# A grouped convolution block on one core: the written orders of every engine and of the DMA queue merged anew

## The chip, the cores and the metric

The kernel runs on one core of a Trainium2 chip. The metric is the device time of one execution in microseconds, lower is better. The engines are TensorE (PE in the profile, its weight loads PEld), VectorE (DVE), ScalarE (ACT), GpSimd (POOL) and SyncE (SP), which here only issues DMAs.

## The reference

The input x is 16 samples of 64 x 64 pixels with 768 channels, f32 (201 MB). Each sample is normalised by groups of channels, projected to 16 channels, convolved by a mixture of four experts whose gates come from the pooled projection, expanded to 768 channels and added to x.

```python
xc = conv1x1(groupnorm(x, 32 groups), conv1_w, conv1_b)        # 768 -> 16 channels
h = mean(xc over pixels) @ H_w.T + H_b                         # 4 gates, the best 2 kept
g = softmax(where(top2, h, -inf))
for i in range(4):                                             # expert i: resize by 2**i, 3x3 conv, resize back
    experts.append(resize(conv3x3(resize(xc, 2**i), convl_w, convl_b), 1))
out = x + conv1x1(sum_i g_i * experts[i], conv2_w, conv2_b)    # 16 -> 768 channels
```

The resizes and the 3x3 convolution fold into one 3x3 convolution with its own taps at the edges. The gates of four samples come together (round r needs samples r, r+4, r+8, r+12 and gives the gates of samples 4r to 4r+3).

## The kernel before

A sample is 8 loads of 1536 KB (`L sample.i:slot`), each into one of 13 slots of `x_sb`; a slot has two halves of 768 KB. x is needed twice: for the statistics and the projection, and again when the result is added. A few loads of eight samples are kept (`KEPT`); the other halves are read a second time (`R sample.i.half:slot.half`). A half is stored by `S sample.i.half`. The queue SP issues the words of `TRANSFERS` one by one and in this order: 128 L, 172 R and 256 S, and waits before each for what it needs. An L or R into a slot whose last tenant was only read waits for PE's transposes of it (`transposed`), into a slot whose tenant was added to it waits until that store has landed (`stored`). An S waits for DVE's adds (`added`).

The work comes in two halves with an order of samples each, `A_ORDER` and `B_ORDER`, which the change leaves alone. A sample enters (A) by these works:

- B on DVE (line 881): statistics of 28 of the 32 groups, in four parts of two loads. S on ACT (lines 786 and 788): the other four groups of each part.
- Z on PE (line 676): four matmuls sum the statistics over the partitions, each once its part is there.
- F on DVE (lines 891 to 911), D on ACT (773): the fold, from the sums to the scaled weights `w1`.
- T on PE (line 651): 24 works of 8 transposes of 128 x 128, from the slots into PSUM; T.5, T.11, T.17 and T.23 free two slots each. T on ACT (line 769): the copy of such a work to SBUF.
- M on PE (line 664): 24 works of 4 matmuls, the projection of one copied work; M.0 waits for `w1`. I on ACT: the image to SBUF.

It leaves (B) by these:

- C on PE (line 716): seven parts of the convolution, with bands of taps that POOL writes. H on ACT and L on DVE: the result in two parts. X on PE and ACT: spread to the partitions.
- E on PE (line 747): 32 tiles of 128 pixels with 768 channels. A on DVE (line 960): the add of such a tile to x.
- G, H, P: the four rounds of gates.

T, E, X, Z and W share a ring of three PSUM buffers, and the copies of T go to three SBUF buffers; so T may run up to six works ahead of M. Every engine runs its works in a written order: `PE_ORDER`, `ACT_ORDER`, `DVE_ORDER`. In a word, `T8.2-5` stands for works 2 to 5 of sample 8. In a bracketed row of the trace a work T is 8 records, a work M is 8 as well, and Z is 8.

```python
            for work in parse_order(PE_ORDER):
                program_of[work[0]](*work[1:])
```

Of the kernel before, what the change touches and what calls it, by code (L numbers as in the profile page):

```python
# [8 lines left out]
ALU = mybir.AluOpType  # L9
# [25 lines left out]


# [23 lines left out]
R0.4.1:11.0 R0.5.0:11.1 R0.5.1:3.0 S0.3.0 S0.3.1 S0.4.0 R0.6.0:3.1 R0.6.1:4.0 R0.7.0:4.1 S0.4.1 S0.5.0 R0.7.1:11.0  # L60
S0.5.1 R4.0.0:11.1 S0.6.0 S0.6.1 R4.0.1:3.0 S0.7.0 R4.1.0:3.1 S0.7.1 R4.1.1:4.0 S4.0.0 R4.2.0:4.1 S4.0.1 R4.2.1:11.0
S4.1.0 R4.3.0:11.1 S4.1.1 R4.3.1:3.0 S4.2.0 R4.4.0:3.1 S4.2.1 R4.4.1:4.0 S4.3.0 R4.5.0:4.1 S4.3.1 R4.5.1:11.0 S4.4.0
R4.6.0:11.1 S4.4.1 R4.6.1:3.0 S4.5.0 R4.7.0:3.1 S4.5.1 R4.7.1:4.0 S4.6.0 S4.6.1 S4.7.0 L14.2:11 S4.7.1 L14.3:3 L14.4:4
S7.0.0 S7.0.1 S7.1.0 S7.1.1 S7.2.0 L14.5:2 S7.2.1 S7.3.0 L14.6:10 S7.3.1 L14.7:12 S7.4.0 S7.4.1 R5.0.0:6.0 S7.5.0
S7.5.1 S7.6.0 S7.6.1 S7.7.0 S7.7.1 L6.0:7 R5.0.1:6.1 S5.0.0 L6.1:1 L6.2:5 L6.3:0 R5.1.0:6.0 S5.0.1 L6.4:10 L6.5:12
R5.1.1:6.1 L6.6:2 L6.7:4 S5.1.0 L10.0:3 L10.1:11 S5.1.1 R5.2.0:6.0 L10.2:8 L10.3:9 R5.2.1:6.1 S5.2.0 L10.4:2 L10.5:4
R5.3.0:6.0 S5.2.1 L10.6:10 L10.7:12 R5.3.1:6.1 S5.3.0 L11.0:0 L11.1:5 R5.4.0:6.0 S5.3.1 L11.2:1 R5.4.1:6.1 S5.4.0
R5.5.0:6.0 S5.4.1 R5.5.1:6.1 S5.5.0 R5.6.0:12.0 R5.6.1:12.1 R5.7.0:6.0 S5.5.1 S5.6.0 S5.6.1 R5.7.1:6.1 S5.7.0
R6.1.0:12.0 R6.1.1:12.1 R6.2.0:6.0 S5.7.1 S6.0.0 S6.0.1 R6.2.1:6.1 S6.1.0 R6.3.0:7.0 S6.1.1 R6.3.1:7.1 S6.2.0
R6.4.0:12.0 S6.2.1 R6.4.1:12.1 S6.3.0 R6.5.0:6.0 S6.3.1 R6.5.1:6.1 R6.6.0:7.0 S6.4.0 R6.6.1:7.1 S6.4.1 S6.5.0 S6.5.1  # L70
R6.7.0:12.0 S6.6.0 R6.7.1:12.1 S6.6.1 L11.3:6 S6.7.0 L11.4:7 S6.7.1 S10.0.0 L11.5:12 S10.0.1 S10.1.0 S10.1.1 L11.6:3
# [917 lines left out]
```

## Time and profile before

| | us |
|---|---|
| median of 3 runs | 1488.0 (1486.47 to 1491.37) |
| the profiled execution | 1492.88 |
| its span, first to last instruction | 1491.2 |
| mean granted TensorE clock | 0.858 |
| moved by DMA | 540.01 MB, mean 362 GB/s |

The profile is of one execution. A row of the windows view gives for a stretch the busy time of PE, PEld, DVE, ACT and POOL, the granted clock of TensorE and the busy share of the DMA engines; a full DMA shows as 1.03, as from 1160 us on. A row of a timeline gives start, length, engine, line, operation and how many; the brackets behind it tell how long the engine sat idle before, and for whom.

### The profile page before, as it was taken

What the parts mean: (1) busy time and instruction counts of PE and PEld (TensorE: products, weight loads), DVE (VectorE), ACT (ScalarE), POOL (GpSimd) and SP (SyncE); (2) the same over time, 40 slices, a digit from 0 to 9 for tenths busy, and PEclk for the clock granted to TensorE, in tenths of its full rate; (3) what the DMA queues carried; (4) which work ended last, traced back from release to release, by engine and by line L of the source; (5) the groups of instructions that cost most, each with busy time, mean ns of one, the idle gap of its engine ahead of it and who ended that gap; (6) DMA issues with size and microseconds to landing.
All of it is one profiled execution on the core that took longest, in us unless ns stands there. A gap on an engine that the chain in (4) does not pass through costs nothing.

```text
span 1491.2 us, 24053 instructions
## 1 busy us (share of the span) xinstructions
PE 1191.8 (80%) x8700; PEld 833.8 (56%) x8700; DVE 1034.0 (69%) x2747; ACT 665.3 (45%) x1549; POOL 313.8 (21%) x381
## 2 busy tenths in 40 slices
PE   0688998998988689889986799879597898876853
PEld 0556776665655466656654577556465565644421
DVE  6778788678559877685496886449685855454843
ACT  2688887672433488625224784403270243100100
POOL 1082003403050000061440001065005003651000
PEclk9899999999997799979977899967798789976855
DMA  9788886499999978999999998999999999999999
GB/s 341 251 336 314 299 304 253 160 409 339 401 384 387 401 288 301 387 368 414 400 393 403 408 389 296 375 411 353 406 382 317 361 413 415 413 415 416 411 406 365
DMA packets 188162, 540.01 MB, mean 362 GB/s; under 512 B 12810, under 2 KB 12810, under 8 KB 188044
## 3 DMA queue, kind: packets, MB, share of 16 engines
q1 hardware_dynamic: 187772, 538.09, 93.7%
q8 instruction: 69, 1.13, 0.3%
q10 hardware_dynamic: 272, 0.39, 0.1%
q14 instruction: 49, 0.40, 0.1%
HBM read 337.12 MB, written 201.33 MB: 361 GB/s over the span
## 4 chain that ended last, share of the span: by engine, by line
PE 40%; DMA 31%; DVE 15%; SPq 5%; ACT 4%; issue 4%; DVEq 0%; ACTq 0%
DMA x_sb<-in_x 22%; PE ring_ps L651 17%; DMA out<-x_sb 9%; DVE x_sb L960 9%; PE img_ps L664 9%; PE conv_ps L716 7%; PE ring_ps L747 5%; DVE stats L881 3%; SPq L483 2%; SPq L493 2%; ACT xT L769 2%; SPq L486 1%; ACT unread_squares L786 1%; ACT unread_copy L788 1%; PE ring_ps L735 1%
## 5 line engine op out<-in xcount | busy, mean ns | idle before, releaser
L960 DVE TENSOR_TENSOR x_sb<-x_sb,ring_ps 128x768 f32<-128x768 f32 x512 | 460.0, 949 | 290.1 <-DMA x_sb<-in_x 165.5
L881 DVE BATCH_NORM_STATS2 stats<-x_sb 128x6 f32<-128x192 f32 x1792 | 474.4, 344 | 65.5 <-DMA x_sb<-in_x 38.7
L769 ACT COPY xT<-ring_ps 128x1024 f32<-128x1024 f32 x384 | 377.3, 1013 | 208.2 <-PE ring_ps L651 175.3
L651 PE MATMUL ring_ps<-ident,x_sb 128*128 128x128 f32 x3072 | 405.5, 291 | 39.2 <-DMA x_sb<-in_x 25.8
L651 PEld LDWEIGHTS ring_ps<-ident,x_sb 128*128 128x128 f32 x3072 | 365.7, 150 | 105.1 <-issue 75.0
L747 PE MATMUL ring_ps<-w,es 128*128 128x512 f32 (+1 forms) x1024 | 324.3, 439 | 95.5 <-DVE x_sb L960 82.5
L747 PEld LDWEIGHTS ring_ps<-w,es 128*128 128x128 f32 x1024 | 190.3, 231 | 207.1 <-DVE x_sb L960 141.7
L664 PE MATMUL img_ps<-xT,w 128*32 128x256 f32 x3072 | 214.6, 399 | 52.4 <-DVE w L911 48.5
L716 PE MATMUL conv_ps<-xc,band 128*128 128x1 f32 (+8 forms) x1120 | 223.4, 346 | 6.6 <-issue 4.3
L614 POOL TENSOR_TENSOR band<-taps,masks 128x640 f32<-128x640 f32 (+1 forms) x112 | 133.0, 1203 | 448.1 <-PE conv_ps L716 444.3
L716 PEld LDWEIGHTS conv_ps<-xc,band 128*128 128x128 f32 x1120 | 160.2, 198 | 78.9 <-issue 72.7
L822 ACT CAST es<-ring_ps 64x1024 fp32r<-64x1024 f32 x64 | 63.3, 1005 | 281.6 <-PE ring_ps L736 281.5
L664 PEld LDWEIGHTS img_ps<-xT,w 128*32 128x32 f32 x3072 | 81.5, 111 | 131.3 <-DVE w L911 52.9
L786 ACT ACTIVATE unread_squares<-x_sb 128x192 bf16<-128x192 f32 x256 | 93.4, 365 | 75.2 <-DMA x_sb<-in_x 43.2
L590 POOL TENSOR_SCALAR taps<-experts,gates 128x400 f32<-128x400 f32 x16 | 20.6, 1287 | 494.0 <-DVE bias_es L945 466.6
L788 ACT ACTIVATE unread_copy<-x_sb 128x192 bf16<-128x192 f32 x256 | 89.7, 350 | 0.0
L810 ACT ACTIVATE es_hi<-conv_ps,bias_es 128x512 fp32r<-128x512 f32 x16 | 11.0, 687 | 154.7 <-PE conv_ps L716 143.9
L676 PE MATMUL ring_ps<-stats,ones 128*128 128x192 f32 x128 | 31.9, 385 | 43.5 <-DVE stats L885 37.2
L735 PE MATMUL ring_ps<-es_hi,pick 32*64 32x512 f32 x128 | 32.0, 527 | 25.3 <-DVE x_sb L960 18.5
L676 PEld LDWEIGHTS ring_ps<-stats,ones 128*128 128x128 f32 x128 | 23.4, 216 | 50.8 <-DVE stats L885 42.3
L786 ACT ACTIVATION_READ_ACCUMULATOR unread_squares<-x_sb 128x1 f32 x256 | 48.8, 190 | 0.0
L788 ACT ACTIVATION_READ_ACCUMULATOR unread_copy<-x_sb 128x1 f32 x256 | 48.5, 189 | 0.0
(94 smaller groups left out, 368.7 us busy)
## 6 DMA issues: line engine op xcount, KB each, us to landing
x_sb<-in_x SPq DMA_DIRECT2D x128, 1536.0 KB, 11.7
out<-x_sb SPq DMA_DIRECT2D x256, 768.0 KB, 12.2
x_sb<-in_x SPq DMA_DIRECT2D x172, 768.0 KB, 13.3
w_rep<-in_L_conv_conv_w ACTq DMA_DIRECT2D x1, 384.0 KB
wl_raw<-in_L_conv_convl_w SPq DMA_DIRECT2D x8, 9.0 KB
gate_w<-in_L_conv_H_w SPq DMA_DIRECT2D x8, 0.2 KB
w_raw<-in_L_conv_conv_w SPq DMA_DIRECT2D x1, 48.0 KB
b_raw<-in_L_conv_conv_b SPq DMA_DIRECT2D x2, 3.0 KB
```

Source lines behind the costliest of these rows:

```text
L614: nc.gpsimd.tensor_tensor(band[:, n % BANDS, :, blocks], taps[:, MAT_ROW_TAP[m]].unsqueeze(2).broadcast_to(full), masks[:, MAT_MASK[m], bl ...
L651: last = nc.tensor.transpose(ring_ps[:, buf, q, half * P:(half + 1) * P], slot("L", a, 2 * c + half)[:, q, k * P:(k + 1) * P], ident[:, :])
L664: last = nc.tensor.matmul(img_ps[32 * q:32 * q + 32, 2 * P * (c % 2):2 * P * (c % 2 + 1)], w1[:, AI[a] % 2, k, R * (1 - c // 2):R * (3 - c ...
L676: nc.tensor.matmul(flat_ps[:, buf, 0:6 * G], ones[:, :], stats[:, c].rearrange("p g t -> p (g t)"), start=(c == 0), stop=(c == CHUNKS - 1) ...
L716: last = nc.tensor.matmul(conv_v[:, blk_out, col_out], band[:, n % BANDS, ax].rearrange("p h r -> p (h r)"), xc_v[:, XC_PLACE[b], blk_in, ...
L747: last = nc.tensor.matmul(flat_ps[:, buf, part], es4[:, q, (i % 4) * P:(i % 4 + 1) * P], w2[:, part], start=True, stop=True)
L769: nc.scalar.copy(xT[:, at % XT], ring_ps[:, TURN["T", a, n] % RING]).then_inc(xT_copied, 1)
L786: nc.scalar.activation(unread_squares[:, :, :].rearrange("p (s q) c -> p s q c", s=2), group, ACT.Square, accum_out=stats[:, c, g, 0:1]).t ...
L788: nc.scalar.activation(unread_copy[:, :, :].rearrange("p (s q) c -> p s q c", s=2), group, ACT.Identity, scale=1.0 / HALF, accum_out=stats ...
L822: nc.scalar.copy(es4[0:64, 2 * half:2 * half + 2, :], halves_ps[0:64, TURN["X", b, part] % RING]).then_inc(es4_ready, 1)
L881: ins = nc.vector.bn_stats(stats[:, c, g, :], two_slots(n0, n1, g))
L960: nc.vector.tensor_tensor(x_sb[:, n, 2 * half + q % 2, :], x_sb[:, n, 2 * half + q % 2, :], flat_ps[:, TURN["E", b, t] % RING, 0:D], ALU.a ...
```

## The change

The tables `TRANSFERS`, `PE_ORDER`, `ACT_ORDER` and `DVE_ORDER` are new. Each holds the same words as before (1482 works on PE, 756 on ACT, 2346 on DVE with each statistics group counted, 556 transfers, with the same slots), in another order; no transfer moves by more than 12 halves of 768 KB. The code around them gains a way to take a sample's last part in two (`SINGLE = 0`: never used) and to run transposes of nothing before M.0 (`WARMED` is empty: never used). The tile `stats` is one part longer, and M.0 waits for its two semaphores in the other order.

```diff
+SINGLE = 0
+
+WARM_UP = 14
+WARMED = set()
...
-S1.0.0 S1.0.1 S1.1.0 L13.5:5 S1.1.1 S1.2.0 S1.2.1 L13.6:2 S1.3.0 S1.3.1 L13.7:3 S1.4.0 S1.4.1 R0.0.0:1.0 S1.5.0 S1.5.1
...
+R2.6.1:8.0 R2.7.0:8.1 L13.0:4 S2.5.0 L13.1:0 R2.7.1:11.1 S2.5.1 S2.6.0 S2.6.1 S2.7.0 L13.2:9 L13.3:8 S2.7.1 S1.0.0
...
-        stats = sb("stats", [P, CHUNKS, G, 6])
+        stats = sb("stats", [P, CHUNKS + 1, G, 6])
...
                 if n == 0:
+                    pe.wait_ge(xc_copied, AI[a])
+                    if a in WARMED:
+                        pe.wait_ge(variance_ready, AI[a] + 1)
+                        for _ in range(WARM_UP):
+                            nc.tensor.transpose(img_ps[:, 0:P], ident[:, :], ident[:, :])
                     pe.wait_ge(w1_ready, AI[a] + 1)
-                    pe.wait_ge(xc_copied, AI[a])
...
-                for c in range(CHUNKS):
-                    pe.wait_ge(stats_taken, AI[a] * CHUNKS + c + 1)
-                    pe.wait_ge(scalar_stats, (AI[a] * CHUNKS + c + 1) * 2 * (G - GV))
+                parts, before = stats_parts(a)
+                for c in range(parts):
+                    pe.wait_ge(stats_taken, before + c + 1)
+                    pe.wait_ge(scalar_stats, (before + c + 1) * 2 * (G - GV))
```

The first place is on PE, from the last works of sample 4 to the first of sample 8. `img_ps<-xT,w` is M (4 to a work), `ring_ps<-ident,x_sb` is T (8 to a work), `ring_ps<-stats,ones` is Z. Before:

```order
L664 MATMUL img_ps<-xT,w 32x256 x8
L651 MATMUL ring_ps<-ident,x_sb 128x128 x16
L664 MATMUL img_ps<-xT,w 32x256 x8
L651 MATMUL ring_ps<-ident,x_sb 128x128 x8
L664 MATMUL img_ps<-xT,w 32x256 x8
L676 MATMUL ring_ps<-stats,ones 128x192 x4
L651 MATMUL ring_ps<-ident,x_sb 128x128 x8
L664 MATMUL img_ps<-xT,w 32x256 x8
L651 MATMUL ring_ps<-ident,x_sb 128x128 x32
```

And now (the lines have other numbers, 697 for 664, 680 for 651, 710 for 676):

```order
L697 MATMUL img_ps<-xT,w 32x256 x12
L680 MATMUL ring_ps<-ident,x_sb 128x128 x24
L697 MATMUL img_ps<-xT,w 32x256 x16
L680 MATMUL ring_ps<-ident,x_sb 128x128 x8
L710 MATMUL ring_ps<-stats,ones 128x192 x4
L680 MATMUL ring_ps<-ident,x_sb 128x128 x24
L697 MATMUL img_ps<-xT,w 32x256 x8
L680 MATMUL ring_ps<-ident,x_sb 128x128 x8
L697 MATMUL img_ps<-xT,w 32x256 x8
```

Two M works of sample 4 and the first T work of sample 8 went from ahead of Z to behind it; before M.0 of sample 8 stand four T works of it, where two stood.

The second place is on PE as well, the end of sample 2's tiles (`ring_ps<-w,es`, two matmuls to a tile) and the convolution of sample 1 (`conv_ps<-xc,band`). Before, the last two tiles, the last two M works of sample 1 and then the convolution:

```order
L747 MATMUL ring_ps<-w,es 128x512
L747 MATMUL ring_ps<-w,es 128x256
L747 MATMUL ring_ps<-w,es 128x512
L747 MATMUL ring_ps<-w,es 128x256
L664 MATMUL img_ps<-xT,w 32x256 x8
L716 MATMUL conv_ps<-xc,band 128x512
L716 MATMUL conv_ps<-xc,band 128x8x63 x2
L716 MATMUL conv_ps<-xc,band 128x8 x2
L716 MATMUL conv_ps<-xc,band 128x64
```

Now, tile 27, the first two parts of the convolution, and tile 28:

```order
L781 MATMUL ring_ps<-w,es 128x512
L781 MATMUL ring_ps<-w,es 128x256
L750 MATMUL conv_ps<-xc,band 128x512
L750 MATMUL conv_ps<-xc,band 128x8x63 x2
L750 MATMUL conv_ps<-xc,band 128x8 x2
L750 MATMUL conv_ps<-xc,band 128x64
L750 MATMUL conv_ps<-xc,band 128x63 x2
L750 MATMUL conv_ps<-xc,band 128x1 x2
L781 MATMUL ring_ps<-w,es 128x512
L781 MATMUL ring_ps<-w,es 128x256
```

The first two parts of the convolution come ahead of tiles 28 and 29, and the other five ahead of tiles 30 and 31; the M works are done before tile 25.

The third place is on SP, where samples 0 and 4 leave, a reload by each store before (L486 is R, L493 is S; the semaphore is that of the slot half which must have been stored):

```order
L493 DMA out<-x_sb 128x2x768 [waits added] x2
L486 DMA x_sb<-in_x 128x2x768 [waits stored3_0]
L493 DMA out<-x_sb 128x2x768 [waits added]
L486 DMA x_sb<-in_x 128x2x768 [waits stored3_1]
L493 DMA out<-x_sb 128x2x768 [waits added]
L486 DMA x_sb<-in_x 128x2x768 [waits stored4_0]
L493 DMA out<-x_sb 128x2x768 [waits added]
L486 DMA x_sb<-in_x 128x2x768 [waits stored4_1]
L493 DMA out<-x_sb 128x2x768 [waits added]
L486 DMA x_sb<-in_x 128x2x768 [waits stored11_0]
```

Now (L515 is R, L522 is S):

```order
L515 DMA x_sb<-in_x 128x2x768 [waits stored3_0]
L522 DMA out<-x_sb 128x2x768 [waits added]
L515 DMA x_sb<-in_x 128x2x768 [waits stored3_1]
L515 DMA x_sb<-in_x 128x2x768 [waits stored4_0]
L515 DMA x_sb<-in_x 128x2x768 [waits stored4_1]
L522 DMA out<-x_sb 128x2x768 [waits added] x3
L515 DMA x_sb<-in_x 128x2x768 [waits stored11_0]
L522 DMA out<-x_sb 128x2x768 [waits added]
L515 DMA x_sb<-in_x 128x2x768 [waits stored11_1]
L522 DMA out<-x_sb 128x2x768 [waits added]
```

Reloads and stores that took turns now stand in small clumps, as the three reloads in a row here.

## Rows read from the trace of the kernel before

**Rows 1.** the page, its busy line

```profile
PE 1191.8 (80%) x8700; PEld 833.8 (56%) x8700; DVE 1034.0 (69%) x2747; ACT 665.3 (45%) x1549; POOL 313.8 (21%) x381
```

**Rows 2.** windows, six stretches (columns: stretch, busy of five engines, clock, DMA share, GB/s)

```profile
0.00:294.00 294.00, 221.88 (x2164) 168.97 (x2164) 223.19 (x874) 208.58 (x550) 75.72 (x151) 0.94 0.76 281
294.00:540.00 246.00, 208.29 (x1548) 145.29 (x1544) 182.92 (x451) 115.03 (x270) 38.51 (x39) 0.88 1.00 385
540.00:600.00 60.00, 52.30 (x537) 40.55 (x536) 50.66 (x204) 50.02 (x132) 0.00 (x0) 0.91 0.75 280
600.00:895.00 295.00, 249.56 (x1897) 177.10 (x1896) 219.43 (x586) 147.14 (x339) 61.54 (x58) 0.87 1.02 395
895.00:1160.00 265.00, 221.16 (x1393) 150.34 (x1392) 168.68 (x375) 90.09 (x191) 71.55 (x70) 0.85 0.96 360
1160.00:1480.00 320.00, 237.63 (x1173) 151.11 (x1171) 186.57 (x259) 54.40 (x72) 66.49 (x64) 0.77 1.03 410
```

**Rows 3.** timeline of PE where samples 0, 4, 8 and 3 begin

```profile
101.05 1.93 PE L664 MATMUL img_ps<-xT,w 128*32 128x256 f32 x16 [4.40 <-DVE w L911]
...
147.40 1.94 PE L664 MATMUL img_ps<-xT,w 128*32 128x256 f32 x16 [4.50 <-DVE w L911]
...
183.12 1.57 PE L676 MATMUL ring_ps<-stats,ones 128*128 128x192 f32 x8
...
189.01 1.07 PE L664 MATMUL img_ps<-xT,w 128*32 128x256 f32 x16 [3.45 <-DVE w L911]
190.01 5.38 PE L651 MATMUL ring_ps<-ident,x_sb 128*128 128x128 f32 x32
...
196.76 2.84 PE L651 MATMUL ring_ps<-ident,x_sb 128*128 128x128 f32 x24
...
229.74 1.07 PE L664 MATMUL img_ps<-xT,w 128*32 128x256 f32 x16 [3.32 <-DVE w L911]
```

**Rows 4.** timeline of DVE across one fold

```profile
178.72 0.24 DVE L885 SCALAR_TENSOR_TENSOR stats<-stats 128x56 f32<-128x56 f32 x1
184.73 0.36 DVE L891 TENSOR_REDUCE small<-ring_ps 128x96 f32<-128x192 f32 x1 [5.77 <-PE ring_ps L676]
...
188.99 7.37 DVE L881 BATCH_NORM_STATS2 stats<-x_sb 128x6 f32<-128x192 f32 x28
...
219.03 0.24 DVE L885 SCALAR_TENSOR_TENSOR stats<-stats 128x56 f32<-128x56 f32 x1
```

**Rows 5.** timeline of ACT, two statistics groups, then three copies

```profile
190.34 0.36 ACT L786 ACTIVATE unread_squares<-x_sb 128x192 bf16<-128x192 f32 x1
...
191.18 0.36 ACT L786 ACTIVATE unread_squares<-x_sb 128x192 bf16<-128x192 f32 x1
...
206.94 2.82 ACT L769 COPY xT<-ring_ps 128x1024 f32<-128x1024 f32 x3
```

**Rows 6.** timeline of the DMA queue, the first stores

```profile
68.52 221.13 SPq L483 DMA_DIRECT2D x_sb<-in_x  x40
294.88 5.56 SPq L493 DMA_DIRECT2D out<-x_sb  x4
```

**Rows 7.** timeline of PE where samples 9 and 5 begin

```profile
544.41 1.93 PE L664 MATMUL img_ps<-xT,w 128*32 128x256 f32 x16 [4.25 <-DVE w L911]
...
585.50 1.27 PE L664 MATMUL img_ps<-xT,w 128*32 128x256 f32 x16 [3.45 <-DVE w L911]
```

**Rows 8.** timeline of PE and DVE, conv of sample 1

```profile
418.17 12.98 PE L716 MATMUL conv_ps<-xc,band 128*128 128x512 f32 x70 [0.90 <-ACT xc L796]
...
430.48 1.92 DVE L881 BATCH_NORM_STATS2 stats<-x_sb 128x6 f32<-128x192 f32 x7 [12.79 <-issue]
```

**Rows 9.** waits of the DMA queue (who waited for whom: us, times, longest)

```profile
SPq L486 <- DMA out<-x_sb: 233.2, 79, 9.2
```

**Rows 10.** windows, where reloads wait for a store close ahead

```profile
902.00:919.00 17.00, 17.00 (x133) 13.07 (x133) 14.20 (x40) 3.94 (x5) 3.81 (x6) 1.00 0.61 207
933.00:953.00 20.00, 17.84 (x141) 11.43 (x139) 11.90 (x14) 7.90 (x8) 0.00 (x0) 0.96 1.01 369
```

More of the change, by code:

```diff
@@ L60 @@
[L60 to L69, printed above, removed]
@@ L442, in pair, with stats_parts, slots_of_part, stats_input @@
             return (loaded[n0], 16 * k0), (loaded[n1], 16 * k1), n0[0], n1[0]
+        def stats_parts(a):
+            of = [CHUNKS + (n < SINGLE) for n in range(AI[a] + 1)]
+            return of[-1], sum(of[:-1])
+        def slots_of_part(a, part):
+            if AI[a] < SINGLE and part >= CHUNKS - 1:
+                return [CHUNKS - 1 + part], True
+            return [2 * part, 2 * part + 1], False
+        def stats_input(a, part, g):
+            which, single = slots_of_part(a, part)
+            waits = [(loaded[loads["L", a, i][0]], 16 * loads["L", a, i][1]) for i in which]
+            places = [loads["L", a, i][0][0] for i in which]
+            if single:
+                return waits, x_sb[:, places[0], :, g * CG:(g + 1) * CG]
+            return waits, two_slots(*places, g)
+        def stats_buffer_free(a, part):
+            before = A_ORDER[AI[a] - 1]
+            return stats_parts(before)[1] + min(part + 1, stats_parts(before)[0])
         def two_slots(n0, n1, g):
@@ L775, in scalar_group @@
             def scalar_group(a, c, g):
[L776 removed]
+                waits, group = stats_input(a, c, g)
+                single = slots_of_part(a, c)[1]
                 if g == GV:
[L778 to L779 removed]
+                    for ready in waits:
+                        act.wait_ge(*ready)
                     if AI[a]:
[L781 to L783 removed]
+                        act.wait_ge(moments_summed, stats_buffer_free(a, c))
+                before = 2 * (G - GV) * (stats_parts(a)[1] + c) + 2 * (g - GV)
                 if before:
                     act.wait_ge(scalar_stats, before)
[L786 to L789 removed]
+                if single:
+                    squares, copies = unread_squares[:, 0:QN, :], unread_copy[:, 0:QN, :]
+                else:
+                    squares = unread_squares[:, :, :].rearrange("p (s q) c -> p s q c", s=2)
+                    copies = unread_copy[:, :, :].rearrange("p (s q) c -> p s q c", s=2)
+                nc.scalar.activation(squares, group, ACT.Square, accum_out=stats[:, c, g, 0:1]
+                                     ).then_inc(scalar_stats, 1)
+                nc.scalar.activation(copies, group, ACT.Identity, scale=1.0 / HALF, accum_out=stats[:, c, g, 1:2]
+                                     ).then_inc(scalar_stats, 1)
             def copy_image(a):
@@ L874, in groups @@
             def groups(a, c, g):
-                one, two, n0, n1 = pair(a, c)
+                waits, group = stats_input(a, c, g)
                 if g == 0:
-                    dve.wait_ge(*one)
-                    dve.wait_ge(*two)
+                    for ready in waits:
+                        dve.wait_ge(*ready)
                     if AI[a]:
-                        dve.wait_ge(moments_summed, (AI[a] - 1) * CHUNKS + c + 1)
-                ins = nc.vector.bn_stats(stats[:, c, g, :], two_slots(n0, n1, g))
+                        dve.wait_ge(moments_summed, stats_buffer_free(a, c))
+                ins = nc.vector.bn_stats(stats[:, c, g, :], group)
                 if g == GV - 1:
```

252 lines of the change are left out of this document (128 added, 124 removed).

## The prediction

> **What bounds the kernel now.** I read the page first. No engine is full: PE is busy for 80% of the span, DVE for 69%, ACT for 45% [rows 1]. Then the windows by stage, for the DMA share. A full DMA shows as 1.03 (1160 to 1480 us). Two stretches fall far below it: 0.76 from 0 to 294 us and 0.75 from 540 to 600 us; 895 to 1160 us stands at 0.96, the others at 1.00 to 1.03 [rows 2]. Lost DMA time is (1.03 - share)/1.03 times the length: 77 us, 7, 16, 3, 18 and 0 for the six stretches, 121 us in all. The transfers are the same before and after and, wherever the DMA is full, the compute has room. So the change is worth what it takes from or adds to these 121 us, and no more.
>
> Who makes the DMA wait in the two poor stretches is seen in the timeline of PE. There samples only enter (T and M works). Samples 0, 4, 8 and 3 each begin with a stall of 4.40, 4.50, 3.45 and 3.32 us, ended by line 911 on DVE, the weights that the fold makes; samples 9 and 5 with 4.25 and 3.45 [rows 3, 7]. After a stall PE runs for a while at its lower level: four T works take 5.38 us at 190.01, but three take 2.84 us at 196.76, so four would take 3.79: 1.6 us lost; and two M works take 1.94 us in place of 1.07, 0.9 us lost [rows 3]. One lap, from M.0 of one sample to M.0 of the next, is 41.6 us (147.40 to 189.01) and 40.7 us (189.01 to 229.74) [rows 3]. A load waits until T has read the slot's old tenant, so the loads go at PE's pace.
>
> The timeline of DVE tells why PE stalls. DVE has the last statistics at 178.96, and then sits idle for 5.77 us until PE has run Z; the fold goes from 184.73 to 188.99, 4.3 us [rows 4]. Z stands in PE's order behind T of the next sample and the last two M works, and only one T stands behind it to cover the fold.
>
> **The change, part by part.** *Z and the T works behind it.* For sample 8 two M works and one T work move from ahead of Z to behind it, and two more T works are drawn ahead of M8.0: in all four T works and two M works follow Z. At 0.95 us for a T (2.84/3) and 0.53 us for an M (1.07/2) they cover 4.9 us [rows 3]: the whole 4.3 us of the fold. The same holds in some measure for 0, 4, 3, 9 and 5. What then bounds a lap? Three engines, nearly alike:
> PE: 24 T at 0.95, 24 M at 0.53, Z with 1.4 (1.57 at 183.12, of which some overlaps) = 36.9 us [rows 3].
> DVE: statistics from 188.99 to 219.27 (219.03 and 0.24) are 30.3 us, fold 4.3, Z between them 1.4 = 36.0 us [rows 4].
> ACT: 24 copies at 0.94 (2.82/3), 16 statistics groups at 0.84 (190.34 to 191.18), some 1.1 for the image and the root = 37.1 us [rows 5].
> So the lap goes from 41.2 (the mean of the two) to no less than 37.1 us; since three engines of almost equal load wait for each other here and there, I take 37.7. In the first stretch the gain of 3.5 us comes in four laps: 14 us (bounds: 0 if ACT or the data hold every lap up, 19.1 if all stalls, 15.7 us, and the surplus of the slower works shown, 0.9 + 0.9 + 1.6 = 3.4 us, go). Between samples 13, 9 and 5 two laps more: 7 us (0 to 10).
> At the head of sample 0 the data set a floor: its last three loads are not issued before 68.52, behind the small weights on SP, in both orders. The first store stands at 294.88 [rows 6]; with 14 us less it comes at about 281.
>
> The Trainium skill has a rule on this (TensorE: Matmul & The Clock Gate, section What's actually happening): the lower level is the default, and activity lifts the engine out of it. The trace agrees, the slow T works follow the stalls. By that rule the surplus goes wholly with the stalls; by the lap sum above, ACT takes that time anyway.
>
> *Conv of sample 1 among the last tiles of sample 2.* Before, all seven parts stand behind the last tile; they take 12.98 us, and DVE sits idle for 12.79 us [rows 8]. Now they stand among the last seven tiles, and the load for which DVE waits there is issued five halves earlier. But DMA stands at 1.00 in this stretch: credited with nothing, bound 0 to 7 us, the loss of the whole stretch.
>
> *The queue of DMA.* 79 waits of line 486 (reloads) for a store are 233.2 us of SP's time [rows 9]. They cost DMA time only where little is queued behind the store. I counted in the two lists, for each of the 230 slot halves that a store empties and a later transfer fills, how many halves (768 KB) lie between the two. None: 2 before, 0 now. One: 10, now 4. Two or three: 39, now 88. Prices: with none between, 902 to 919 us, which holds the only two, shows a share of 0.61, a loss of 6.9 us, 3.5 each; with two between, 933 to 953 us shows 1.01, a loss of 0.4 us over its three such waits, at most 0.2 each [rows 10]. For one between no row is clean; I take 1.5, inside 0.2 and 3.5. Gain: 6.9 + 6 x 1.5 = 16 us; loss: 49 x 0.2 = 10 us. Sum: 6 us to the good; of that I take 4, since the bound from below is nothing gained and late adds share in the same loss.
>
> The Trainium skill (DMA: Bandwidth & Descriptors, section Anatomy of one DMA — SWDGE (gpsimd) path) gives about 2.0 us of fixed cost for each DMA, most of it completion. By that figure one 768 KB half in between would nearly hide a wait, and the loss of 10 us would be close to none.
>
> Sum: 14 + 7 + 0 + 4 = 25 us. The profiled execution took 1492.88 us, so 1468; the median of the three runs is 1488.0, and against it the forecast is **1463 us**.
>
> **The rivals.**
> *The laps stay (chance 0.09).* ACT or late data hold each lap at about 40 us: ACT's orders now have single statistics groups between copies, each of which waits for its own load, and a copy behind it then waits too. For it: ACT is the fullest by my sum, 37.1 us. Against: in the groups shown it is never late, and PE has up to six works in buffers. Gain 4 laps x 1 + 2 x 1 + 4 = 10 us: 1478.
> *Given back at the full DMA (chance 0.09).* The stores begin 14 us earlier, but the middle stretch, where conv, tiles and adds are interleaved anew, loses as much: 1488. For it: 294 to 540 us has no slack in the DMA, and a store out of step costs at once. Against: PE is busy for 208 of 246 us there, so there is room.
> *The clumped queue (chance 0.12), slower.* The reloads now stand in clumps of three or four with the stores in a clump behind. In these clumps each reload waits for a store two or three halves ahead. If such a wait costs 1.0 us and not 0.2, the 49 more cost 49 us: less 16 and 21 gained, that is 12 us slower, 1500. It decides from (21 + 16)/49 = 0.76 us each. For it: 233.2 us of such waits already [rows 9]. Against: the 0.2 of 933 to 953 us.
>
> **How the numbers follow.** The likeliest has 0.70: its own range is 1463 less 12 (all stalls and surplus gone, and the middle stretch's loss halved) and plus 12 (half of the laps' gain): 1451 to 1475. About 0.3% (4.5 us) is what a measurement of this kernel can tell from no change. The range that leaves out no more than 2 in 10 takes in the two rivals up to 1488: **1448 to 1489**. Faster by over 0.3%: 0.70, 0.08 from the first rival, a little from the second: 0.78. Within 0.3%: 0.10. Slower: 0.12.
>
> **What the profile after would show.** In the timeline of PE the stalls for line 911 are under 1 us for 4, 8, 3, 9 and 5, and a lap is 37 to 38 us; the four T works at each head take 3.8 us. DVE's wait ahead of line 891 is under 2 us. The DMA share of the first 280 us is about 0.80. The first store is issued at 277 to 284 us. For 294 to 540 and 600 to 895 us the share stays at 1.00 or above; a fall to 0.95 there would be 12 to 14 us and would show the second rival. Waits for stores with DMA below full would show the third. I would be wrong, too, if ACT were idle in those stretches for DMA, or if PE stood at Z for the statistics for more than 2 us in a lap.

## The result, and the profile after

The changed kernel takes **1467.33 us** (median of 4 runs, 1463.79 to 1469.02), against 1487.24 us (4 runs, 1485.14 to 1491.37) for the kernel before: a ratio of 0.986, 95% interval 0.9831 to 0.9888. That is 20 us less. The profiled execution is the quickest of its four, and the one of before was slower than that kernel's median: the spans are 1462.1 and 1491.2 us, 29.1 apart. Where the text below speaks of single places it goes by the profiles; 20 us is the size of the effect.

The page's busy line of the kernel after answers to [rows 1]. PE, DVE and ACT have the same work. DVE and ACT spend about the same time on it, PE 14 us more (the ends of its matmuls are modelled, so this is rough); what shrank is the time around the work.

```profile
PE 1206.2 (82%) x8700; PEld 818.7 (56%) x8700; DVE 1028.5 (70%) x2747; ACT 661.6 (45%) x1549; POOL 314.9 (22%) x381
```

The windows of the kernel after, cut where the same six stages end now, with the columns of [rows 2]:

```profile
0.00:276.00 276.00, 218.87 (x2165) 160.81 (x2166) 225.15 (x874) 202.98 (x535) 72.76 (x149) 0.98 0.83 305
276.00:516.00 240.00, 211.62 (x1543) 144.73 (x1543) 178.12 (x450) 117.22 (x282) 42.47 (x41) 0.90 1.00 383
516.00:572.00 56.00, 53.45 (x585) 40.48 (x587) 51.30 (x207) 46.62 (x105) 0.00 (x0) 1.00 0.95 357
572.00:858.00 286.00, 249.91 (x1816) 171.05 (x1808) 208.75 (x548) 142.79 (x342) 61.63 (x58) 0.87 1.01 384
858.00:1133.00 275.00, 228.59 (x1407) 151.59 (x1406) 182.47 (x405) 90.67 (x180) 66.55 (x64) 0.84 1.00 373
1133.00:1450.00 317.00, 243.76 (x1194) 150.08 (x1193) 180.84 (x264) 61.30 (x108) 71.53 (x70) 0.81 1.03 405
```

The two poor stretches have filled up: 0.76 has become 0.83, and 0.75 has become 0.95; 0.96 has become 1.00. By the same formula as in the prediction the lost DMA time is 54, 7, 4, 6, 8 and 0 us, 79 in all, where it was 121. Note that 42 us less were lost and the span fell by 29 only; the last section comes back to the other 13.

The timeline of PE in the kernel after, at the heads of samples 4, 8 and 3, answers to [rows 3]. Line 710 is Z, 680 is T (8 matmuls to a work), 697 is M (8 to a work):

```profile
134.92 1.57 PE L710 MATMUL ring_ps<-stats,ones 128*128 128x192 f32 x8
...
137.86 3.71 PE L680 MATMUL ring_ps<-ident,x_sb 128*128 128x128 f32 x32
141.50 1.73 PE L697 MATMUL img_ps<-xT,w 128*32 128x256 f32 x24
...
171.98 1.47 PE L710 MATMUL ring_ps<-stats,ones 128*128 128x192 f32 x8
173.28 2.78 PE L680 MATMUL ring_ps<-ident,x_sb 128*128 128x128 f32 x24
...
178.02 0.64 PE L697 MATMUL img_ps<-xT,w 128*32 128x256 f32 x8
...
215.17 1.07 PE L697 MATMUL img_ps<-xT,w 128*32 128x256 f32 x16
217.56 0.64 PE L697 MATMUL img_ps<-xT,w 128*32 128x256 f32 x8 [1.33 <-ACT xT L803]
```

No stall for the weights is left; a wait of 1.33 us for a copy on ACT is the largest shown here (the longest from 100 to 240 us is 1.6 us). The laps, from one sample's first M work to the next one's, are 36.5 us (141.50 to 178.02) and 37.2 us (178.02 to 215.17), where they were 41.6 and 40.7. The timeline of ACT and then of DVE after Z of sample 4 shows why. Line 807 is the root in the fold (the D work), 803 a T copy, 825 and 827 the two halves of a statistics group:

```profile
137.39 1.01 ACT L803 COPY xT<-ring_ps 128x1024 f32<-128x1024 f32 x1 [0.91 <-PE ring_ps L680]
138.30 0.23 ACT L807 ACTIVATE norm<-norm 128x32 f32<-128x32 f32 x1
...
139.10 1.01 ACT L803 COPY xT<-ring_ps 128x1024 f32<-128x1024 f32 x1
139.99 0.38 ACT L825 ACTIVATE unread_squares<-x_sb 128x192 bf16<-128x192 f32 x1
...
140.84 0.36 ACT L825 ACTIVATE unread_squares<-x_sb 128x192 bf16<-128x192 f32 x1
...
141.54 3.76 ACT L803 COPY xT<-ring_ps 128x1024 f32<-128x1024 f32 x4
```

```profile
136.52 0.36 DVE L935 TENSOR_REDUCE small<-ring_ps 128x96 f32<-128x192 f32 x1 [1.05 <-PE ring_ps L710]
```

DVE waits 1.05 us for Z of sample 4, where it waited 5.16. For samples 0, 8 and 3 it waits 2.58, 2.25 and 1.97 us, where it waited 3.11, 5.77 [rows 4] and 6.19. ACT does the root right behind one copy and has only two statistics groups to do before four more copies. In the timeline of the DMA queue the first store goes out 19.0 us earlier than in [rows 6]:

```profile
275.92 4.30 SPq L522 DMA_DIRECT2D out<-x_sb  x3
```

The waits of the DMA queue over the whole kernel after, for reloads behind a store, answer to [rows 9]:

```profile
SPq L515 <- DMA out<-x_sb: 281.8, 85, 10.6
```

The queue waits 48.6 us more for its stores than before, yet the DMA share where this happens is 1.00 and 1.01. So these waits of SP lie beside a full DMA.

**Two places, and something given back.** A good ruler is the moment at which DVE takes the gates of a round, which happens four times in the kernel. Its timeline in the kernel before has the second and third gate (`gates<-ring_ps`):

```profile
636.32 0.14 DVE L943 TENSOR_SCALAR gates<-ring_ps 128x16 f32<-128x16 f32 x1
...
972.65 0.16 DVE L943 TENSOR_SCALAR gates<-ring_ps 128x16 f32<-128x16 f32 x1
```

and in the kernel after:

```profile
602.12 0.17 DVE L987 TENSOR_SCALAR gates<-ring_ps 128x16 f32<-128x16 f32 x1 [1.58 <-PE ring_ps L735]
...
939.39 0.17 DVE L987 TENSOR_SCALAR gates<-ring_ps 128x16 f32<-128x16 f32 x1 [0.70 <-PE ring_ps L735]
```

The first and the last of the four are at 237.2 and 1249.7 us before, at 220.2 and 1216.9 after. So the change gains 17.0 us up to the first gate and 17.2 between the first and the second; from the second to the third it loses 0.9, to the last 0.4, and behind the last one it loses 3.7 (241.5 us become 245.2).

### The profile page after: what moved, and what is told of

It is laid out like the page before. It is cut to its first block, busy times and chain, and to the rows that moved or that the text cites. A ratio compares the mean times of both kernels' runs of the same rounds, so it can differ in the third digit from the quotient of the medians.

```text
span 1462.1 us, 24056 instructions
## 1 busy us (share of the span) xinstructions
PE 1206.2 (82%) x8700; PEld 818.7 (56%) x8700; DVE 1028.5 (70%) x2747; ACT 661.6 (45%) x1549; POOL 314.9 (22%) x381
## 3 DMA queue, kind: packets, MB, share of 16 engines
q1 hardware_dynamic: 187772, 538.09, 96.4%
## 4 chain that ended last, share of the span: by engine, by line
PE 43%; DMA 28%; DVE 13%; ACT 6%; SPq 5%; issue 4%; POOL 1%; DVEq 0%; ACTq 0%; POOLq 0%
PE ring_ps L680 15%; DMA x_sb<-in_x 14%; DMA out<-x_sb 14%; PE conv_ps L750 10%; DVE x_sb L1004 9%; PE ring_ps L781 8%; PE img_ps L697 8%; SPq L512 3%; ACT xT L803 3%; DVE stats L920 2%; SPq L483 1%; PE ring_ps L769 1%; ACT unread_copy L827 1%; ACT unread_squares L825 1%; PE ring_ps L710 1%
## 5 line engine op out<-in xcount | busy, mean ns | idle before, releaser
L680 PE MATMUL ring_ps<-ident,x_sb 128*128 128x128 f32 x3072 | 399.8, 283 | 66.8 <-DMA x_sb<-in_x 25.4
L680 PEld LDWEIGHTS ring_ps<-ident,x_sb 128*128 128x128 f32 x3072 | 348.7, 145 | 146.4 <-issue 89.4
L781 PE MATMUL ring_ps<-w,es 128*128 128x512 f32 (+1 forms) x1024 | 334.5, 443 | 111.7 <-DVE x_sb L1004 84.4
L750 PE MATMUL conv_ps<-xc,band 128*128 128x1 f32 (+8 forms) x1120 | 235.1, 360 | 4.0 <-issue 2.7
L697 PE MATMUL img_ps<-xT,w 128*32 128x256 f32 x3072 | 218.4, 393 | 16.9 <-ACT xT L803 13.2
L750 PEld LDWEIGHTS conv_ps<-xc,band 128*128 128x128 f32 x1120 | 168.0, 207 | 79.0 <-issue 76.2
L697 PEld LDWEIGHTS img_ps<-xT,w 128*32 128x32 f32 x3072 | 77.2, 110 | 97.5 <-issue 39.0
L621 POOL TENSOR_SCALAR band<-experts,gates 128x400 f32<-128x400 f32 x32 | 41.1, 1286 | 3.1
L623 POOL TENSOR_TENSOR taps<-taps,band 128x400 f32<-128x400 f32 x32 | 33.2, 1038 | 2.7
```

Of the source, the lines that this page charges most:

```text
L680: last = nc.tensor.transpose(ring_ps[:, buf, q, half * P:(half + 1) * P], slot("L", a, 2 * c + half)[:, q, k * P:(k + 1) * P], ident[:, :])
L697: last = nc.tensor.matmul(img_ps[32 * q:32 * q + 32, 2 * P * (c % 2):2 * P * (c % 2 + 1)], w1[:, AI[a] % 2, k, R * (1 - c // 2):R * (3 - c ...
L750: last = nc.tensor.matmul(conv_v[:, blk_out, col_out], band[:, n % BANDS, ax].rearrange("p h r -> p (h r)"), xc_v[:, XC_PLACE[b], blk_in, ...
L781: last = nc.tensor.matmul(flat_ps[:, buf, part], es4[:, q, (i % 4) * P:(i % 4 + 1) * P], w2[:, part], start=True, stop=True)
```

## The experiments

All twelve kernels have the code of the changed kernel and differ in the four tables alone; "of before" means the tables. Each was timed in one of three groups together with the kernel before, whose medians there were 1488.35 us (experiments 1 to 4), 1489.90 (5 to 8) and 1488.31 (9 to 12). The ratios and the differences to the kernel before go by these; a difference between two experiments of different groups, or to the changed kernel's 1467.33, is less sure by a microsecond or two. Line numbers differ by one or two from kernel to kernel, since the tables wrap differently. Where two tables of different origin meet, one goes on with its own order, leaving out the works already done.

**1. The queue's order alone.** All engine orders of before, and

```diff
-S3.0.0 S3.0.1 S3.1.0 S3.1.1 R3.2.0:4.0 R3.2.1:4.1 R3.3.0:0.0 L1.5:6
+S3.0.0 S3.0.1 S3.1.0 R3.2.0:4.0 S3.1.1 R3.2.1:4.1 R3.3.0:0.0 R3.3.1:0.1
...
```

> The kernel before with only the order of the DMA queue taken from the changed kernel; all engine orders are those of before. Theory A (the laps carry the change, the queue's order is a small term): 4 us of the 20, so 1483 us (1479 to 1487), first store still at 293 to 296 us. Rival B (clumps of reloads and stores are dangerous by themselves): above 1492 us. Rival C (the 12.4 us more packet time that the changed kernel shows per DMA engine is made by the queue's order): the mean 3072-byte packet goes from 127.0 ns to 128.0 or more, and the time is 1490 or more.

Measured: 1530.01 us, ratio 1.0279 (1.0256 to 1.0302). 42 us slower than before. Theory A's small term of 4 us is refuted as a thing of its own; B and C both forecast the direction. By the gates, 13.8 us are lost between the first and the second gate and 21.8 between the second and the third. Over the whole kernel the queue stands 101 us longer before its stores for adds that DVE has not done yet. The waits of SP in the kernel before, then in this one:

```profile
SPq L493 <- DVE x_sb L960: 300.4, 171, 8.1
```

```profile
SPq L523 <- DVE x_sb L1005: 401.4, 178, 11.2
```

Rival C's other sign came as well: the packets took 1412 us of each DMA engine's time, 15 more than before (last section). But that is not the whole loss, and experiment 2 shows the same with the queue's order of before.

**2. The engines' orders alone.** The reverse: the changed kernel with

```diff
-R2.6.1:8.0 R2.7.0:8.1 L13.0:4 S2.5.0 L13.1:0 R2.7.1:11.1 S2.5.1 S2.6.0 S2.6.1 S2.7.0 L13.2:9 L13.3:8 S2.7.1 S1.0.0
+R2.6.1:8.0 R2.7.0:8.1 S2.5.0 R2.7.1:11.1 L13.0:4 S2.5.1 S2.6.0 S2.6.1 S2.7.0 L13.1:0 S2.7.1 L13.2:9 L13.3:8 L13.4:11
...
```

> The changed kernel with only the order of the DMA queue put back to that of before. Theory A: the laps before the first store stay at 37 us, the first store comes at about 276 us, and the time is 1471 us (1467 to 1476), 4 us above the changed kernel. Rival C (the queue's order costs packet time): packets back at 127.0 ns and about 12 us less than the changed kernel, 1455 to 1460 us. Rival D (engine and queue orders were written for one another and a mixture waits): 1480 us or more, with new waits of the queue above 3 us.

Measured: 1515.27 us, ratio 1.018 (1.0155 to 1.0206): Rival D, 27 us slower than before. C falls: the packets took 1411 us and not 1397. The waits of SP for adds, 382.4 us in the changed kernel, are

```profile
SPq L522 <- DVE x_sb L1004: 476.7, 187, 16.7
```

The timeline of the DMA queue shows the longest of them, before the loads of sample 13:

```profile
405.09 1.08 SPq L512 DMA_DIRECT2D x_sb<-in_x  x1
422.80 0.37 SPq L522 DMA_DIRECT2D out<-x_sb  x1
423.27 4.29 SPq L512 DMA_DIRECT2D x_sb<-in_x  x3
```

and DVE's timeline over the same time:

```profile
414.84 5.55 DVE L920 BATCH_NORM_STATS2 stats<-x_sb 128x6 f32<-128x192 f32 x21 [10.25 <-issue]
...
420.96 1.81 DVE L1004 TENSOR_TENSOR x_sb<-x_sb,ring_ps 128x768 f32<-128x768 f32 x2
```

The queue stands for 16.6 us before the last store of sample 2. DVE in its new order takes 21 statistics of sample 13 first and only then the last two adds of sample 2. Those statistics need `L13.1`, which in the queue's order of before goes out only at 405.09; DVE is idle for 10.25 us until 414.84. In the changed table `L13.1` stands five transfers earlier, and `L13.2` and `L13.3` go ahead of the store, too. Both halves of the change are needed here, and over the whole kernel each alone is worse than none. This place is one of several: against the changed kernel 22.7 us are lost between the first and the second gate, where it lies, 19.0 between the second and the third, and 7.9 behind that. Of those later losses no single place was traced, nor of those in experiment 1.

**3. The first stretch alone.** Before, with the engine orders of the change up to the last M of sample 3 (the queue as before; on DVE this moves nothing but the work G0):

```diff
-M4.20-21 T8.0 M4.22-23 Z8 T8.1 M8.0-1 T8.2-5 M8.2-4
+M4.18-21 T4.23 Z8 T8.0-2 M4.22-23 T8.3 M8.0-1 T8.4-5 M8.2-4
```

> The kernel before, with the engine orders of the changed kernel up to the last M work of sample 3 and nothing else. Theory A (the gain is made in the laps before the first store): first store at 275 to 279 us, and 14 us of the 20, so 1473 us (1469 to 1478). Rival (given back at a full DMA): first store as early, and the time within 5 us of before, 1482 or more. If packets are slower because the stores begin earlier, the mean packet is 127.5 ns or more here.

Measured: 1474.10 us, ratio 0.9898 (0.9876 to 0.9919), 14 us less than before, as theory A had it. The first gate is at 219.8 us and the last at 1233.3: the 17.4 us of the first gate are still 16.5 at the last one and in the span. What was gained before the first store stayed gained. In the timeline of the queue the first store is at

```profile
278.12 5.56 SPq L524 DMA_DIRECT2D out<-x_sb  x4
```

**4. The first stretch undone.** The same edit the other way round, in the changed kernel.

> The changed kernel, with the engine orders of before up to the last M work of sample 3 and nothing else undone. Theory A: first store at 290 to 296 us, and of the 20 us some 6 stay, so 1481 us (1477 to 1485). Rival (the gain is spread over the later laps and the queue, the first stretch is given back): 1473 us or less.

Measured: 1482.40 us, ratio 0.9953 (0.9931 to 0.9975), 6 us less than before, as theory A had it. Its twelve runs lie wide, from 1474.74 to 1490.70 us. The 14 of experiment 3 and these 6 make the 20; the section on the prediction shows that the 6 are themselves a gain and a loss.

**5. Behind the last gate undone.** The changed kernel, and from the last gate on

```diff
 R8.5.1:1.0 R8.6.0:1.1
-R8.6.1:7.1 R8.7.0:0.0 R8.7.1:0.1 R14.0.0:5.0 S8.3.1 S8.4.0 S8.4.1
+S8.3.1 R8.6.1:7.1 S8.4.0 R8.7.0:0.0 R8.7.1:0.1 S8.4.1 R14.0.0:5.0
...
```

> The changed kernel with the four orders of before behind the last gate (from the 433rd transfer on in the queue). In the profiles the stretch from the last gate to the end took 240.6, 240.8 and 241.1 us with the engine orders of before, and 243.4, 244.6 and 246.0 with those of the change. Theory A (the change gives some 4 us back behind the last gate): 4 us less than the changed kernel's 1467, so 1463 us (1460 to 1466), and 241 us behind the last gate. Rival (those 4 us are what the DMA engines still have to move): 1467, and 244 us or more behind the gate.

Measured: 1464.07 us, ratio 0.9827 (0.9795 to 0.9858), 3 us under the changed kernel. From the last gate (1222.6) to the end of the span (1465.0) it is 242.4 us against 245.2. The size and the place are those of theory A, but the intervals of the two kernels' ratios overlap, so it isn't settled.

**6. The change up to the second gate, before behind it.**

```diff
 S0.3.1 R0.5.1:3.0
-R0.6.0:3.1 S0.4.0 S0.4.1 R0.6.1:4.0 S0.5.0 R0.7.0:4.1
+S0.4.0 R0.6.0:3.1 R0.6.1:4.0 R0.7.0:4.1 S0.4.1 S0.5.0
...
```

> The four orders of the changed kernel up to the second gate (180 transfers in the queue), those of before behind it. Theory A (the change gains in two places, 17 us before the first store and 17 us between the first and the second gate, and loses 4 us behind the last one): second gate at 601 to 605 us as in the changed kernel, 33 us less than before by the profile, 1455 us (1452 to 1460). Rival (what was gained in between is given back once the DMA engines are full, whatever the order): the distance from the second gate to the end grows from 854 to 862 us or more, and the time is 1465 or more.

Measured: 1464.31 us, ratio 0.9837 (0.9808 to 0.9866). Neither expectation holds whole. From the second gate to the end it is 854.9 us (609.63 to 1464.5), as in the kernel before, so nothing is given back there. But the second gate comes 7.5 us later than in the changed kernel. DVE's timeline has it behind a long wait for TensorE, where the changed kernel has 1.58 us:

```profile
609.63 0.17 DVE L989 TENSOR_SCALAR gates<-ring_ps 128x16 f32<-128x16 f32 x1 [9.22 <-PE ring_ps L737]
```

TensorE in turn waits for a copy on ACT, and ACT has eleven statistics groups in one block ahead of that copy, from 596.88 to 606.05 us. The timeline of PE, and that of ACT with the first and the last group of the block:

```profile
607.09 1.97 PE L682 MATMUL ring_ps<-ident,x_sb 128*128 128x128 f32 x8 [10.12 <-ACT xT L805]
```

```profile
596.88 0.35 ACT L827 ACTIVATE unread_squares<-x_sb 128x192 bf16<-128x192 f32 x1
...
605.34 0.36 ACT L827 ACTIVATE unread_squares<-x_sb 128x192 bf16<-128x192 f32 x1
...
606.05 0.99 ACT L805 COPY xT<-ring_ps 128x1024 f32<-128x1024 f32 x1
```

The block is in neither kernel's table. It is the seam: of the works that the order of before still had to do, eleven groups came to stand between `P1` and `T7.0`, where the change has two and before has `T7.0` ahead of `P1`.

**7. TensorE's order alone, in the first stretch.** The edit of experiment 3 on PE only; on ACT just

```diff
-T0.0 I12 T0.1 S0.3.31 S4.0.28-30 D0 S4.0.31 S4.1.28-31 T0.2-7
+S0.3.31 T0.0 I12 T0.1 S4.0.28-30 D0 S4.0.31 S4.1.28-31 T0.2-7
```

> The kernel before with only TensorE's order of the changed kernel up to the last M work of sample 3 (and one ACT work, the last statistics of sample 0, moved ahead of one T work so that TensorE gets on). ACT's order stays with whole blocks of statistics of the next sample ahead of the T copies. Theory A (the laps are long because Z stands behind works of the next lap on TensorE): laps of 37 to 38 us, first store at 276 to 280 us, 1475 us (1472 to 1479). Rival (ACT's order is the other half: its statistics hold back the T copies and the scale of the sample at hand): laps of 40 us or more, first store at 287 us or later, 1482 us or more.

Measured: 1506.80 us, ratio 1.0124 (1.0095 to 1.0154). Not only is nothing gained, it is 17 us slower than before, and the first store goes out at 309.6 us. Theory A in this form falls and the rival holds. DVE's waits from 100 to 240 us say what came in the stall's place:

```profile
DVE norm L943 <- ACT norm L808: 22.2, 4, 5.9
```

In the middle of the fold DVE waits for ACT's root, 22.2 us in four waits, where it was 2.9 in three. Z ran earlier, so the fold wants its root earlier, but the root (`D4`, say) stands on ACT where it stood: behind a second T copy and three statistics groups of the next sample.

**8. ACT's order alone, in the first stretch.**

```diff
-T0.0 I12 T0.1 S0.3.31 S4.0.28-30 D0 S4.0.31 S4.1.28-31 T0.2-7
+S0.3.30-31 T12.21-23 S4.0.28 D0 T0.0-1 I12 S4.0.29 T0.2 S4.0.30-31 T0.3-7
...
```

> The kernel before with only ACT's order of the changed kernel up to the last T copy of sample 3. Theory A (TensorE's order alone makes the laps): first store at 292 to 296 us and 1487 us (1484 to 1490). Rival (ACT's order carries at least a third of the gain): first store at 289 us or earlier, 1483 us or less.

Measured: 1493.42 us, ratio 1.0035 (1.0013 to 1.0057), first store at 297.0 us. Nothing gained by ACT alone, rather 4 us lost: theory A in kind, 3 us above its range.

**9. TensorE's order and the roots.** As 7, and besides

```diff
-T4.0 I0 T4.1 S8.0.28-30 D4 S8.0.31 S8.1.28-31 T4.2-11
+T4.0 D4 I0 T4.1 S8.0.28-31 S8.1.28-31 T4.2-11
...
```

> TensorE's order of the changed kernel up to the last M work of sample 3, as in the run with that alone, and now also ACT's square roots (the D works of samples 0, 4, 8 and 3) right behind the first T copy of their sample; the statistics of the next sample and the T copies stay in blocks as before. Theory A (TensorE's order was right and 22 us were lost because the root stood behind seven or eight statistics works on ACT): no wait of DVE for ACT's norm above 1.5 us, weights of sample 3 ready at 214 to 219 us, first store at 276 to 281 us, 1476 us (1472 to 1480). Rival (the blocks of statistics in front of the T copies cost by themselves): weights of sample 3 at 224 us or later, 1483 us or more.

Measured: 1509.33 us, ratio 1.0144 (1.0116 to 1.0171): the Rival. The wait for the root did go (4.3 us in three), and the time did not move. The timeline of PE at the head of sample 4:

```profile
145.01 3.71 PE L681 MATMUL ring_ps<-ident,x_sb 128*128 128x128 f32 x32
148.66 1.07 PE L698 MATMUL img_ps<-xT,w 128*32 128x256 f32 x16
154.81 1.08 PE L698 MATMUL img_ps<-xT,w 128*32 128x256 f32 x8 [5.09 <-ACT xT L804]
```

and that of ACT over the same time, the first and the last of its eight statistics groups and the copies behind them:

```profile
147.14 0.38 ACT L826 ACTIVATE unread_squares<-x_sb 128x192 bf16<-128x192 f32 x1
...
153.06 0.36 ACT L826 ACTIVATE unread_squares<-x_sb 128x192 bf16<-128x192 f32 x1
...
153.77 2.82 ACT L804 COPY xT<-ring_ps 128x1024 f32<-128x1024 f32 x3
```

The four T works run behind Z and cover the fold (the weights are there at 148.66), but M4.2 needs the copy of T4.2, and ACT does eight groups first, from 147.14 to 153.77, 6.6 us. In the kernel before this block cost nothing: it lay beside the stall of PE. With the stall gone, the block is the stall: from 100 to 240 us PE waits 16.4 us for copies, where it waited 15.7 us for the weights in the kernel before. What the change does on ACT is to cut the block up. Why the kernel is slower than before, and not just as slow, was not traced.

**10. The cover taken away.** Experiment 3, but at the heads of samples 0, 4 and 8 the T works are moved out from between Z and M.0:

```diff
-Z4 T4.0 M0.23 T4.1-4 M4.0-2
+T4.0-1 Z4 M0.23 M4.0-1 T4.2-4 M4.2
...
```

> The kernel with the first stretch of the change alone (1474 us), and in it the T works that stood between Z and the first M work of samples 0, 4 and 8 moved: two ahead of Z, the others behind the first two M works. Theory A (these T works cover the fold of DVE's 4.3 us): stalls of 2 us or more for w return at three heads, three laps of 2 to 3.7 us more, first store 6 to 11 us later than 276, 1483 us (1480 to 1486). Rival (the floors of the lap lie elsewhere, in ACT's copies and statistics, and TensorE catches up behind the stall): first store within 3 us, 1477 us or less.

Measured: 1487.09 us, ratio 0.9986 (0.9969 to 1.0002), 13.0 us above experiment 3: 4.3 us to a head. The time is 1 us above theory A's range; its signs came. The timeline of PE at samples 4 and 8:

```profile
145.04 1.94 PE L699 MATMUL img_ps<-xT,w 128*32 128x256 f32 x16 [3.18 <-DVE w L957]
...
186.75 0.64 PE L699 MATMUL img_ps<-xT,w 128*32 128x256 f32 x8 [2.75 <-DVE w L957]
```

The stall of before is back, with the slow pair of M works behind it at sample 4 (1.94 us), and the first store goes out at 289.08 us, 11.0 later. The edit does two things at once: it takes T works away from behind Z, and it puts Z itself behind two of them, so that DVE's waits for Z from 100 to 240 us rise from 5.3 to 13.9 us. So, where ACT's order allows it, an early Z with T works behind it is worth 13 us at these three heads; the two parts were not taken apart.

**11. The change up to the third gate, before behind it.**

```diff
 S6.5.1 R6.7.0:12.0
-R6.7.1:12.1 L11.3:6 S6.6.0 S6.6.1 S6.7.0 S6.7.1 L11.4:7
+S6.6.0 R6.7.1:12.1 S6.6.1 L11.3:6 S6.7.0 L11.4:7 S6.7.1
...
```

> The orders of the changed kernel up to the third gate (322 transfers), those of before behind it. From the profiles: third gate at 937 to 940 us, then 275 to 277 us to the last gate and 240 to 241 us to the end with the orders of before, so a span of 1453 to 1458. Theory A (pieces add up): 1458 us (1455 to 1462). Rival (each seam costs some us, as the one at the second gate did with 7): 1463 us or more.

Measured: 1465.42 us, ratio 0.9844 (0.9821 to 0.9867). The pieces don't add up; the rival holds. The third gate comes at 941.8 us, 2.4 later than in the changed kernel; from there to the last gate it is 280.5 us, where the orders of before took 274.7 to 277.1, and to the end 241.9. So what the end gives is lost around the seam. No cause was traced here.

**12. No cover at samples 9 and 5.** The changed kernel with

```diff
-Z9 T9.2-5 M9.0-2
+Z9 M9.0-1 T9.2-5 M9.2
...
-T5.0 Z5 M9.21-23 T5.1-5 M5.0-2
+T5.0-1 Z5 M9.21-23 T5.2 M5.0-1 T5.3-5 M5.2
```

> The changed kernel with the T works between Z and the first M work of samples 9 and 5 moved as far ahead of Z or behind the first two M works as ACT's order lets them. Theory A (the second 17 us are the same cure as the first ones: DMA's hole at 500 to 600 us closes because the heads of samples 9 and 5 no longer stall): second gate 7 to 15 us later than 602.8, 1477 us (1473 to 1482). Rival (it is the queue's order and the other T and M works in these laps that close the hole): second gate within 3 us, 1470 us or less.

Measured: 1471.75 us, ratio 0.9895 (0.9872 to 0.9918), 4.4 us above the changed kernel; the second gate is at 607.74 us, 5.6 later. Between the two expectations: the cover at these heads is a third of the 17.2 us gained there. The rest must be in another place, and no run takes it away alone; the traces show where it may be. The waits of PE in the kernel before, from 486 to 616 us, have it first:

```profile
PE ring_ps L676 <- DVE stats L885: 14.0, 2, 7.5
PE img_ps L664 <- DVE w L911: 11.4, 3, 4.3
```

and in the kernel after, from 470 to 585 us:

```profile
PE ring_ps L710 <- DVE stats L929: 0.7, 1, 0.7
```

At 481 us PE stood ready at Z of sample 13 and waited 14.0 us for that sample's last two blocks of statistics. DVE was not idle then: it took those blocks from 482.68 to 495.79 us, behind adds. In the changed order it takes them earlier, among the adds of samples 2, 1 and 0, and their loads come earlier in the queue. In experiment 2, which has DVE's new order and the queue of before, PE waits at this Z for 0.21 us only, and yet the stretch between the gates is 404.7 us long, 5.6 more than before: the wait has moved to the place shown there.

## Why the prediction was right

**The time.** 1463 us were forecast and 1467 measured, 25 us less against 20. The first part of the sum was right in size and, with the condition below, in mechanism. That the whole came so near is partly luck: by the gates the second stretch gained 17 us and not the 7 of the heads, and the change lost some microseconds behind the third gate that the sum did not have.

**Z and the T works behind it: 14 us.** Right in sum. The place of M3.0 moved from 229.74 to 215.17, 14.6 us; experiment 3 gives 14 us of the median, and experiment 10 shows that it is Z's place and the T works behind it: 13.0 us for three heads. The four laps gained 1.7, 4.2, 5.1 and 3.6 us, where the sum had 3.5 in each. Most signs came as forecast: laps of 36.5 and 37.2 us for "37 to 38", four T works in 3.71 us for 3.8, no stall for the weights, a DMA share of 0.83 for 0.80, the first store at 275.9, just below 277 to 284. DVE's wait for Z was forecast under 2 us and is so at two of the four heads (1.05 and 1.97 us, 2.25 and 2.58 at the others). The lap of 36.5 us lies under the 37.1 that the sum called ACT's floor, so that floor was some 0.6 us too high. What the step lacked is its condition. It took ACT for a floor of 37.1 us per lap, a sum of its work, and looked at PE's order for the gain. Experiments 7 and 9 show that the order on ACT is half of the change: with PE's order alone the kernel is 17 us slower, with the roots moved too it is no better. The prediction has a rival in which ACT holds the laps, but nothing on what ACT's old order would do to the new order of PE. The first rival had the right engine (ACT late by its statistics groups) with the wrong sign: single groups between the copies are the cure and not the risk, since what hurts is a block of them (8 groups in experiment 9, 11 in experiment 6). In the changed kernel ACT waits for no load at all from 100 to 240 us.

**Samples 9 and 5: 7 us.** The term of the cover is 4.4 us by experiment 12, inside 0 to 10. But the stretch as a whole gave 17.2 us by the gates, and the row that seems to have the greater part was not read: the wait of PE at Z of sample 13, 14.0 us; the rows read were those of the next two heads [rows 7]. The windows did hold some of it, as a share below full [rows 2]; the prediction put the whole of it down to the heads.

**Conv of sample 1: 0.** Not tested by itself. DVE's idle time of 12.79 us there is gone in the changed kernel, and experiment 2 has 10.25 us at the same place; it belongs to the piece just named.

**The queue's order: 4 us.** The step that failed in kind. The sum priced the queue by itself, by distances between a store and its reload. Experiment 1 shows +42 us for it alone, experiment 2 +27 us for all else without it. It has no price of its own; its partner are the engines' orders, DVE's in the place shown. No run tests the prices by the number of halves between, nor the fixed cost of a DMA that the prediction quoted beside them. The rival of the clumped queue did not come about in the changed kernel: 85 waits for a store, at a share of 1.00 and 1.01.

**Given back at the full DMA.** This rival had a chance of 0.09, and a part of it came true. The middle did not give back (0.9 us between the second and the third gate). Behind the last gate 3.7 us went, and experiment 5 may get 3 of them back. Between the third and the last gate the changed orders took 277.5 us in the profiled execution of the changed kernel, its quickest, but 282.2, 285.9 and 288.5 in those of experiments 12, 5 and 4, which have the same orders in that stretch. With the orders of before it took 274.7 to 277.1 us in before and in experiments 3 and 6 to 10. So the stretch that costs 0.4 us in the two profiles costs 5 to 11 in the other three; this may be why the profiles are 29 us apart and the medians 20. It is also why experiment 4 keeps 6 us only, though its second gate comes 18.7 us sooner behind the first than before. The DMA was at a share of 1.01 in all four, and moved 389 GB/s in the quickest against 384, 380 and 381; so it is again the time of the packets and no idle DMA. Why is open.

The Trainium skill says that TensorE runs at its lower level unless activity lifts it (TensorE: Matmul & The Clock Gate, section What's actually happening). The runs agree: as the stalls went, the granted clock of the first stretch rose from 0.94 to 0.98, and experiment 10 has part of both back, with 0.96 up to its first store, a stall of 3.18 us, and two M works behind it in 1.94 us instead of 1.07.

## What to carry to other kernels

When a stall is taken away, ask what has been lying beside it for nothing. Here it was a block of 6.6 us on ACT, and the cure on PE alone made the kernel slower. Orders of several engines and of a queue that were made together have to be judged together: neither the queue's table nor the engines' tables as a whole have a gain of their own, though the engines' orders up to the first store do (14 us), where the queue's order is the same in both kernels. A seam between two good orders cost 7.5 us, because it stacked eleven works on one engine. And of time gained, look where it was gained: nearly all that came before the first store was still there at the end.

## What the hardware showed that was not expected

The lost DMA time fell by 42 us and the span by 29. The rest is in the packets themselves. The DMA queue in the page of the kernel before, then of the kernel after (packets, MB, share of 16 engines' span):

```profile
q1 hardware_dynamic: 187772, 538.09, 93.7%
```

```profile
q1 hardware_dynamic: 187772, 538.09, 96.4%
```

The same packets and bytes, yet 93.7% of 1491.2 us is 1397 us of each engine's time, and 96.4% of 1462.1 is 1409: 12 us more. The windows between the second and the third gate, of before and then of after, show it at work:

```profile
636.90:973.30 336.40, 290.90 (x2176) 205.28 (x2176) 241.61 (x614) 158.49 (x339) 66.61 (x64) 0.89 0.99 383
```

```profile
602.80:940.00 337.20, 298.85 (x2166) 205.24 (x2167) 236.69 (x601) 164.36 (x382) 66.62 (x64) 0.88 1.00 377
```

A share of 0.99 moved 383 GB/s, a share of 1.00 moved 377. Over all runs this goes with the orders behind the second gate: 1395 to 1400 us where all four are those of before (before, experiments 3, 6, 7, 8, 9 and 10), 1409 to 1413 in the changed kernel and in experiments 1, 2, 4, 5 and 12, where some or all are those of the change, and 1406 in experiment 11, which changes over at the third gate. It alone did not set the time: experiment 5 with 1412 us and experiment 6 with 1400 ran in 1464.07 and 1464.31. So a share near 1.00 doesn't mean that the DMA engines move as much as they can, and a sum of the time lost by the share, as the prediction made it, leaves out some 12 us in this kernel. The queue's order alone (experiment 1) and the engines' orders alone (experiment 2) each bring the longer time. What lengthens the packets was not found.
